# Running each engine one group further ahead in a routed-expert layer

## What is computed

```python
logits = _gelu(xf @ router_w1 + router_b1) @ router_w2 + router_b2     # top 2 of 8 experts
for _ in range(2):
    ctx = concatenate([integrated, v], -1)
    shared_ctrl = _gelu(ctx @ shared_w1 + shared_b1) @ shared_w2 + shared_b2
    x_sh, v_sh = _inl(shared_ctrl, integrated, v, mu)
    ctrl = _experts(ctx_e, flat_idx, expert_w1, expert_b1, expert_w2, expert_b2)
    x_r, v_r = _inl(ctrl, x_e, v_e, mu)              # weighted sum over the 2 experts
    halt = sigmoid(_gelu(integrated @ halt_w1 + halt_b1) @ halt_w2 + halt_b2)
    x_next, v_next = sw * x_sh + (1 - sw) * x_r, sw * v_sh + (1 - sw) * v_r
    integrated, v = integrated + halt * (x_next - integrated), v + halt * (v_next - v)
refined = _gelu(integrated @ refine_w1 + refine_b1) @ refine_w2 + refine_b2
# _inl: a, b, g = split(ctrl, 3); v' = sigmoid(a) * v - softplus(b) * (x - mu); x' = x + 0.1 * sigmoid(g) * v'
```

## Time and profile before

| what | value |
|---|---|
| median of 3 runs | 1744.98 us (1744.79 to 1745.25) |
| the profiled execution's own time | 1741.15 us |
| its span, first to last instruction | 1739.2 us |
| busy: PE, DVE, ACT, POOL | 62%, 61%, 49%, 41% |
| mean granted TensorE clock | 0.798 of full speed |
| DMA, mean | 103 GB/s |

### The profile page before, as it was taken

The page is one execution under the profiler, slowest core; times in us unless marked ns, Lnnn a source line. Parts: engine busy times, 40 slices in busy tenths (PEclk is TensorE's granted clock), DMA queues, the critical chain, the costliest instruction groups (busy, mean ns, idle before and its releaser), DMA issues.

```text
span 1739.2 us, 21709 instructions
## 1 busy us (share of the span) xinstructions
PE 1085.2 (62%) x6930; PEld 648.3 (37%) x6930; DVE 1057.5 (61%) x1951; ACT 845.1 (49%) x1303; POOL 720.3 (41%) x692
## 2 busy tenths in 40 slices
PE   4778887978989456521556551654546666644775
PEld 2334453544544233200423231332225555532443
DVE  1655656666665337566465553888756777764665
ACT  1134534444545334354556652643547777751544
POOL 6012322223223360176233435645266666437451
PEclk9678988998989867665677775876768988876888
DMA  4946357176270395023243424544143333214341
GB/s 88 147 69 104 67 87 118 39 97 106 65 87 14 82 250 180 15 98 115 76 137 110 137 94 146 193 145 134 37 121 97 110 110 110 62 52 139 98 120 59
DMA packets 151755, 178.84 MB, mean 103 GB/s; under 512 B 33207, under 2 KB 127826, under 8 KB 151517
## 3 DMA queue, kind: packets, MB, share of 16 engines
q1 hardware_dynamic: 134624, 124.85, 31.6%
q0 software_dynamic: 17024, 52.58, 10.0%
HBM read 100.25 MB, written 76.87 MB: 102 GB/s over the span
## 4 chain that ended last, share of the span: by engine, by line
DVE 20%; PE 15%; ACT 13%; issue 10%; POOL 5%; DMA 2%; SPq 0%; ACTq 0%; DVEq 0%; POOLq 0%
PE exp_ps L1966 7%; DVE h_hl L1571 4%; ACT ct L1455 3%; DVE xs L1809 2%; DVE vs L1810 2%; PE exp_ps L2055 2%; ACT ct L1445 2%; PE exp_ps L2057 2%; ACT g L1413 1%; PE exp_ps L2056 1%; DVE h_h L1570 1%; ACT L1466 1%; PE exp_ps L2016 1%; DVE ct L1725 1%; ACT h_hl L1414 1%
## 5 line engine op out<-in xcount | busy, mean ns | idle before, releaser
L561 DVE TENSOR_REDUCE neg_max<-att_ps 128x1 f32<-128x512 f32 (+3 forms) x448 | 217.0, 533 | 75.5 <-PE att_ps L730 74.1
L499 ACT ACTIVATE probs<-att_ps 128x512 f32<-128x512 f32 x320 | 175.8, 609 | 172.1 <-PE att_ps L739 171.2
L1300 POOL TENSOR_TENSOR rb<-rb,ct 128x1024 f32<-128x1024 f32 x44 | 108.7, 2471 | 329.4 <-ACT ct L1465 329.4
L729 PE MATMUL att_ps<-k_stack,q_stack 96*128 96x512 bf16 (+3 forms) x512 | 163.3, 360 | 70.5 <-DVE neg_max L561 31.9
L1966 PE MATMUL exp_ps<-w_top,h_hl 128*128 (+2 forms) x280 | 102.1, 428 | 135.6 <-DVE h_hl L1571 117.7
L1399 ACT CAST e_xT<-exp_ps 128x512 f16<-128x512 f32 x172 | 92.5, 607 | 130.3 <-PE exp_ps L1944 130.1
L2055 PE MATMUL exp_ps<-e_xT,w 128*128 128x128 f16 x432 | 112.4, 266 | 57.0 <-issue 56.3
L406 POOL TENSOR_TENSOR wait_carrier<-wait_carrier 128x1 f32<-128x1 f32 x64 | 12.5, 195 | 297.4 <-ACT probs L499 297.4
L739 PE MATMUL att_ps<-q_stack,k_stack 98*128 98x512 bf16 (+3 forms) x512 | 125.4, 319 | 9.4 <-DMA q_stack<-max_parts 7.3
L730 PE MATMUL att_ps<-mask_q,identb 128*128 128x128 bf16 x512 | 126.5, 253 | 0.0
L1564 DVE TENSOR_TENSOR e_xT<-exp_ps,e_xT 128x512 f16<-128x512 f32 x172 | 109.8, 684 | 19.6 <-ACT e_xT L1399 18.2
(11 more groups left out here) (269 smaller groups left out, 3033.2 us busy)
## 6 DMA issues: line engine op xcount, KB each, us to landing
rs_dram<-rb SPq DMA_DIRECT2D x18, 1024.0 KB, 4.9
parts_dram<-parts SPq DMA_DIRECT2D x48, 256.0 KB, 2.6
q_stack<-parts_dram SPq DMA_DIRECT2D x96, 128.0 KB, 6.3
k_stack<-parts_dram SPq DMA_DIRECT2D x96, 128.0 KB, 9.9
xs_dram<-zeros SPq DMA_DIRECT2D x18, 520.0 KB, 9.8
xg<-xs_dram SPq DMA_DIRECT2D x18, 520.0 KB, 6.0
rs_dram<-rb SPq DMA_DIRECT2D x18, 512.0 KB, 2.9
x_in<-in_L_attn_encodings SPq DMA_DIRECT2D x8, 512.0 KB, 10.6
```

Source lines behind the costliest of these rows:

```text
L499: nc.scalar.activation(probs[:, pair % 4, u, :], src, ACT.Exp).then_inc(free, 1)
L561: return v.tensor_reduce(out, scores, AX.X, ALU.max, negate=True)
L729: t_.matmul(out, stationary, moving, start=True, stop=False)
L1300: g_.tensor_tensor(m, m, b, ALU.subtract).then_inc(pool_step, 1)
```

## The change

The order of the work on each engine is moved by one item. PE's order becomes hidden n+1, control n, turn n+2; ACT's gelu n+1, tanh n, casts n+2, logarithm n; DVE's split n+1, update n-1, absolute n, low parts n+2 (in B: relu and absolute n before update n-1). `h_hl` and `h_h1` get two buffers, and `FILLS` the new order. C and D become one loop, so that the first quads of D are turned and multiplied while the last groups of C are updated. POOL gathers three groups ahead in C (two before), and issues the gathers of D's first three quads between the products of the groups 4 to 6 of C. PE's halt logits move behind the control product. In E the turn and the first layer of group g+1 move around the second layer of group g in the same manner, and the statistics of a group follow its residual at once. The diff, cut to its core:

```diff
-        h_hl = sb("h_hl", [P, TOK], F16)
-        h_h1 = sb("h_h1", [P, TOK], F16)
+        h_hl = sb("h_hl", [P, 2, TOK], F16)
+        h_h1 = sb("h_h1", [P, 2, TOK], F16)
...
+        for first, end in ((W_B, W_S2), (W_S2, EWS)):
+            FILLS += turn_fills(first) + hidden_fills(first) + turn_fills(first + 1)
+            for n in range(first, end):
+                FILLS += hidden_fills(n + 1) if n + 1 < end else []
+                FILLS += turn_fills(n + 2) if n + 2 < end else []
...
             def gather_state(q):
+                if q == 0:
+                    for g in range(GROUPS):
+                        pool.wait_ge(xv_stored[g], 32)
+                    pool.wait_ge(comb_done, TILES)
...
+            for t in range(3 * NT):
+                gather1(t)
             for g in range(GROUPS):
-                pool.wait_ge(xv_stored[g], 32)
-            pool.wait_ge(comb_done, TILES)
-            AHEAD = D_RING - 2
-            for q in range(AHEAD):
-                gather_state(q)
+                for t in range((g + 3) * NT, min((g + 4) * NT, TILES)):
+                    gather1(t)
+                products(W_S2 + g, xs[:, g * NT:(g + 1) * NT, 0:D])
+                if GROUPS - 4 <= g < GROUPS - 1:
+                    gather_state(g - (GROUPS - 4))
+            gather_state(3)
             for q in range(QUADS):
                 products(W_D + q, xg_it2(q)[:, :, 0:D])
-                if q + AHEAD < QUADS:
-                    gather_state(q + AHEAD)
+                if q == 0:
+                    gather_state(4)
+                if q + 5 < QUADS:
+                    gather_state(q + 5)
...
+            for first, end in ((W_B, W_S2), (W_S2, EWS)):
+                turned(first)
+                hidden(first)
+                turned(first + 1)
+                for n in range(first, end):
+                    if n + 1 < end:
+                        hidden(n + 1)
+                    tanhs(n)
+                    if n + 2 < end:
+                        turned(n + 2)
+                    if W_S2 <= n < W_D:
+                        halt_gate(n - W_S2)
+                    logs(n)
...
             act.wait_ge(ew_done, EWS)
+            casts("e", 0, KC)
             for g in range(GROUPS):
-                casts("e", g, KC)
-                if g:
-                    act.wait_ge(ctrl_filled[(uses(EWS) + g - 1) % 2], (uses(EWS) + g - 1) // 2 + 1)
-                    rstd(g - 1)
                 for c in range(RC):
                     src, free = filled(f"eh{g}_{c}")
                     s.activation(gr32[:, c, :], src, ACT.Gelu, bias=cols[:, 2 + c:3 + c])
                     s.activation(gp[:, 0, c, :], src, ACT.Gelu, bias=cols[:, 2 + c:3 + c]).then_inc(free, 1)
+                if g + 1 < GROUPS:
+                    casts("e", g + 1, KC)
+                if g:
+                    rstd(g - 1)
...
+            for n in range(W_S2, EWS):
+                if n + 1 < EWS:
+                    hidden2(n + 1)
+                if n > W_S2:
+                    update2(n - 1)
+                absolute(n)
+                if n + 2 < EWS:
+                    turned2(n + 2)
+                if n + 3 < W_D:
+                    combine1(n + 3 - W_S2)
+            update2(EWS - 1)
...
             for g in range(GROUPS):
-                if g:
-                    lows("e", g, KC)
-                    steps = spread_of(g - 1)
                 refine_low(g)
+                if g + 1 < GROUPS:
+                    lows("e", g + 1, KC)
                 if g:
                     finish(g - 1, steps)
                 if g + 2 < GROUPS:
                     combine2(g + 2)
                 take(g)
-            finish(GROUPS - 1, spread_of(GROUPS - 1))
+                steps = spread_of(g)
+            finish(GROUPS - 1, steps)
...
+            for first, end in ((W_B, W_S2), (W_S2, EWS)):
+                turn_stage(first)
+                at = stage_hidden(first)
+                if first == W_S2:
+                    halt_logits(0)
+                turn_stage(first + 1)
+                for n in range(first, end):
+                    here = at
+                    if n + 1 < end:
+                        at = stage_hidden(n + 1)
+                    control(n, h_hl[:, n % 2], h_h1[:, n % 2], here)
+                    if W_S2 <= n + 1 < W_D and n + 1 < end:
+                        halt_logits(n + 1 - W_S2)
+                    if n + 2 < end:
+                        turn_stage(n + 2)
...
+            turn_refined(0)
+            refine_hidden(0)
+            for g in range(GROUPS):
+                if g + 1 < GROUPS:
+                    turn_refined(g + 1)
+                refine_out(g)
+                if g + 1 < GROUPS:
+                    refine_hidden(g + 1)
```

195 lines of the change are left out of this document (81 added, 114 removed).

## The result

The changed kernel takes 1635.65 us (median of four runs, 1632.6 to 1638.91), against 1744.88 us for the kernel before in the same rounds. The ratio is **0.939, with a 95% interval of 0.9366 to 0.9414**: faster. The forecast was 1642 us.

The account below looks back on a forecast made before the run. No engine is full, so rings of waits were taken to bound each stage. Terms -34 - 29 - 24 + 0 - 16 = -103 took 1741.15 to 1638, or 1642 us in the median; range 1612 to 1690, about 8 in 10.

Parts of the forecast that it names:

- the drains of B and D: Ends of stages B and D: emptying costs about 3 us more in B and some 6 in D.
- B, -34: 18 quads, first iteration: ring from hidden product through control, tanh, update, low parts falls from 12.79 to 10.5 us; -34 us.
- The store in B with "about 1 us to spare": Sign of being wrong: ACT waits for a store before its tanh, a ring through SP counted as hidden.
- C, -29: 8 groups, second iteration, shared expert: turn falls from 24.85 to 20.2 us, set by DVE; -29, between -13 and -32.
- The passage, -24: From C to D: PE's 18.68 us wait for the first gather goes, 58.4 us become 33.5; 24 counted.
- D, 0 (-6 + 6): 18 quads, second iteration: turn 14.1 against 14.5 us saves 6, the drain costs some 6; between +11 and -13.
- E, -16: 8 groups, refinement: next group's gelus done during gather waits, 4.7 us less per ring of two groups; -16, between -10 and -20.
- The way to B, 0: Start of the program to the first quad of B: forecast difference 0 us.
- Rival 1: Whole kernel: PE stays at the 1.2 GHz level after pauses, sum -44, so 1701 us; chance 0.14.
- Rival 2: B and D: POOL's two products fall on DVE's ring, up to 4.84 us per quad, sum +71, 1816 us; chance 0.05.
- Rivals 3 and 4: 3: PE faster through most of a group, 1612 us, chance 0.09; 4: nothing moves, 1745 us, chance 0.02.

Follow-up runs that it names:

- The first experiment: On the changed kernel, DVE took the low parts of item n+2 ahead of the update of item n-1 in B and D: 1684.67 us.
- fillers: On the changed kernel, PE ran products of constants that nothing reads while waiting for the next quad's low parts in B and D: 1621.43 us.
- The experiment with the fixed expert: On the kernel with parted update, later halt logits, E's gathers ahead and fillers (1591.42 us), D's hidden products used expert 0's weights at fixed addresses: 1574.1 us.

## Why the prediction was right, point by point

The forecast of 1642 stands 6 us from 1635.65. Against the profiled execution it was a sum of -103 where -108.6 came. The steady turns of B, C and D came as laid out; the two ends of the stages did not. The terms that came out better than forecast (the drains of B and D, E, the way to B) make 29 us, those that came out worse (C's filling, C with the passage, D's turns) 24. That they nearly cancel, and the total is so close, is luck.

- **B, -34; measured -44.6.** The ring was the right one, link by link. The hidden product takes the slow stretch: 2.95 us for 2.96 (921.10 to 924.05). The control product took about 2.1, for which I had chosen 2.4; the turn is 10.24 for 10.5. The first fifteen turns brought 37.1 us, as much as was forecast for the turns. The rest is the drain, priced at +3, which brought a gain of 7.5: the last two turns were 9.4 and 8.7 us, where they were 12.8 and 12.9 before. The first has no low parts left in it, and the second no hidden product either.
- **The store in B with "about 1 us to spare".** The page gives 4.9 us from the store's issue to its landing; issued at 929.96 it lands at about 934.9, and the tanh that needs it starts at 925.41 + 10.24 = 935.65. The first experiment shows this ring closed when the update comes 1.2 us later.
- **C, -29; measured about -24, turns right, ends not priced.** The five full turns are 19.7 to 21.4 us, 20.7 in the mean for 20.2, and bring 21 of 23 us; the two turns of the ramp bring 3 of 6. DVE works without a gap but for the halt logits, 0.92 us, which I had named as what could eat the gain. What the sum left out is the filling. One item more ahead means that a second group's low parts and hidden product stand in front of C's first tanh, which starts 46.9 us after B's last mark (1010.48 to 1057.35) for 40.8 before (1058.92 to 1099.75), and the casts of the third group come between that tanh and the logarithm. So C's first product on POOL starts 55.8 us after B's last, not 47.5: **+8.4 us in a term that the sum put at nothing**.
- **The passage, -24; measured -21.** The gather is there in time: issued until 1168.4, turned at 1180.1, and moved by a whole turn it costs 2.5 us. From the last hidden product of C to the second of D it is 37.1 us for 33.5. The first of the two steps is 20.6 where I had 17.5; in it DVE waits 2.63 us for halt logits that PE multiplies behind the last control product.
- **D, 0 (-6 + 6); measured -6.5.** The turn of 14.1 was right for eleven of the fourteen inner turns, 14.2 in the mean. The other three took 15.0 to 15.1, so the mean of all is 14.37, for 14.46 before; the first turn is 1.6 us longer. So the turns gave nothing (+0.3) where 6 were forecast, although DVE is busy for 40 us less. The drain is the largest single error of the forecast: +6, and the last two turns are 6.8 us shorter than before.
- **E, -16; measured -18.1.** Two groups take 35.0 us for 33, since DVE still waits 7.31 us for gathers in every second group; the first normalisation comes 59.3 us after D's last mark, 64.2 before, which I had hardly counted. With E's order undone, the stretch is 22.0 us longer.
- **The way to B, 0; measured -3.9.** Nothing is changed there; the mark moves by up to 15 us from kernel to kernel.

**Rival 1, the clock.** After each pause PE does run at the 1.2 GHz level, and in some turns of D through the whole hidden product. With fillers, which raise the granted clock from 0.83 to 0.98 in B (870 to 1000) and from 0.86 to 0.96 in D (1230 to 1440), the gain is 7.1 us in B and 2.3 in D. The experiment with the fixed expert shows why it is so little: with addresses from registers a burst takes about 0.09 us a product even at the full clock. That is a mean over the burst and no floor for two products in a row. In the turn of D above, 14 products start 0.055 us apart (1327.28 to 1328.00) once the clock has risen, behind 3 us at the 1.2 GHz level, and the last start 0.06 to 0.13 us apart. The burst takes 4.54 us all the same, as it does with the clock full throughout (4.55). This looks as if the products of the slow stretch had been made ready ahead of their start, which no run tests. Only where the whole burst runs at the 1.2 GHz level does it take longer, 5.41 us (from 1352.26). The Trainium skill (TensorE: Matmul & The Clock Gate, section HAM oscillation) says that bursts with waits between them lose the full clock and pay for it in every burst. The traces agree on the loss of the clock, but not on its weight here: taken as the whole story it gave a sum of -44, and -108.6 came; the fillers bring back about 9 us in B and D. In C and E no run holds the clock up.

**Rival 2, POOL on DVE's ring.** The mechanism is real and near: POOL ends 0.04 us before DVE's copy in B and 0.87 in D (1326.71 + 2.35 to 1329.93). That the logarithm hangs on the same ring and keeps POOL in its place was right. One more operation on POOL costs 48 us, a later update 45. The Trainium skill (SBUF — State Buffer, section Who interferes with whom) describes an exclusive lock that is held for a whole instruction, counts copies among the instructions that can meet it, and says that whoever issues first has it. The traces agree: the copy took 1.51 us in place of 0.28, and where DVE came first it was POOL that took 3.10 in place of 2.34.

**Rivals 3 and 4.** The faster level through most of a group did not come (B reached rival 3's -43 through its drain, not through the clock); that the orders took effect is plain in the rows of B.

## What to carry to other kernels

Lay the rows of one turn end to end for each stage, with the lookahead as it will be: the steady turns came out within 3% in B, C and D, and 6% too short in E, where a wait for gathers stayed. Then price the two ends of each stage apart from its turns: going one item further ahead delayed C's first result by 8.4 us, by what stands in front of it now, and shortened the drains of B and D by 7.5 and 6.8, where less is left to do. Before an operation is moved off a ring, ask who waits for its store and what shares a port with it at its new place: here moving the update looked like 40 us to be saved in B and D, and cost 45.

## What had not been expected of the hardware

- A burst of 52 products of 128 columns whose weights stand at addresses from registers took 4.55 us from the first start to the last at the granted clock of 1.00, 0.089 a product, and 2.84 us at fixed addresses, 0.056 a product. At the 1.2 GHz level throughout it took 5.41 us, 0.106 a product, so with addresses from registers the full clock saves 0.9 us of 5.4. A burst that starts at the slower level and ends at the faster one was as short (4.54 us).
- When DVE came first (the run with the update behind), POOL's operations of 128x1024 took 3.1 to 3.2 us in place of 2.34, and DVE's next one then 3.25 in place of 1.23: the two hand their waits back and forth.
- The untouched first half of the program took 833.9 to 849.0 us in executions that differ only behind it.
